# Attention rows of blocks 8 to 31 turned by DMA transposes of 16-bit halves

## The reference

```python
mod = (silu(c) @ wmod).reshape(2, 6, 1, 512)          # sa, ca, ga, sb, cb, gb
h = layernorm(x) * (1 + ca) + sa
q, k, v = silu(h @ wq), sigmoid(h @ wk), h @ wv         # 4 heads of 128
f = 1 - k;  g = log(f);  theta = cumsum(sign(f - 0.5)) * pi
S_t = S_(t-1) * exp(g_t) + k_t v_t;  o_t = (q_t * scale) S_t     # q and k times cos/sin(theta)
o = layernorm(o * sigmoid(h @ wg1 @ wg2)) * norm_w
x = x + ga * (o @ wo)
h = layernorm(x) * (1 + cb) + sb
xr, xk = mixes of h and of h one row earlier, by mu_r and mu_k
x = x + gb * sigmoid(xr @ W_r) * (square(relu(xk @ W_k)) @ W_v)
```

## Time and profile before

| | us |
|---|---|
| median of 3 runs | 1760.68 |
| lowest and highest | 1760.49, 1760.76 |
| profiled execution | 1760.39 |
| span of its instructions | 1758.6 |
| TensorE busy | 1736.2 |
| VectorE busy | 1544.2 |
| ScalarE busy | 905.6 |
| GpSimd busy | 409.2 |

### The profile page before, as it was taken

The page is one execution under the profiler, slowest core; times in us unless marked ns, Lnnn a source line. Parts: engine busy times, 40 slices in busy tenths (PEclk is TensorE's granted clock), DMA queues, the critical chain, the costliest instruction groups (busy, mean ns, idle before and its releaser), DMA issues.

```text
span 1758.6 us, 45285 instructions
## 1 busy us (share of the span) xinstructions
PE 1736.2 (99%) x18677; PEld 1559.8 (89%) x18677; DVE 1544.2 (88%) x3483; ACT 905.6 (51%) x1551; POOL 409.2 (23%) x361
## 2 busy tenths in 40 slices
PE   9999999999999999999999999998999999999999
PEld 7888989998999989999999989987788888888888
DVE  7898988998999989998989989898888888888885
ACT  4444444445444445444444444444566666666664
POOL 1000101101011011110111001101455555555552
PEclk9999999999999999999999999999999999999999
DMA  6122112211122111321112111121343332333331
GB/s 240 48 64 61 38 37 68 67 38 38 37 44 67 38 38 41 103 53 37 38 44 55 50 38 38 44 68 37 96 108 93 88 109 85 96 106 86 97 88 45
DMA packets 168949, 117.22 MB, mean 67 GB/s; under 512 B 126996, under 2 KB 128808, under 8 KB 168744
## 3 DMA queue, kind: packets, MB, share of 16 engines
q1 hardware_dynamic: 168728, 114.33, 24.6%
q10 hardware_dynamic: 16, 0.00, 0.0%
HBM read 48.77 MB, written 34.60 MB: 47 GB/s over the span
## 4 chain that ended last, share of the span: by engine, by line
PE 94%; DVE 5%; issue 1%; ACT 0%; DMA 0%; POOL 0%; SPq 0%; DVEq 0%; ACTq 0%
PE bank L1410 65%; PE lvl L1410 9%; PE bank L1517 3%; PE bank L1524 3%; PE bank L1516 3%; PE lvl L1485 3%; PE bank L1418 2%; PE bank L1508 1%; PE lvl L1468 1%; PE lvl L1503 1%; PE lvl L1497 1%; PE bank L1743 0%; DVE xn L139 0%; PE bank L1736 0%; DVE xk L1062 0%
## 5 line engine op out<-in xcount | busy, mean ns | idle before, releaser
L133 POOL TENSOR_TENSOR ln_rs<-ln_ve,mhalf 128x2 f32<-128x2 f32 x64 | 82.5, 1289 | 616.8 <-DVE ln_ve L128 616.6
L434 POOL COPY og_halves<-og 128x1024 uint16<-128x1024 uint16 x60 | 65.7, 1095 | 407.5 <-DVE og L1018 407.5
L1410 PE MATMUL bank<-xk_hi,fk_hi 128*128 128x256 f32 x512 | 145.8, 285 | 4.7 <-DVE xk_lo L1075 4.7
L1410 PE MATMUL bank<-hT_hi,wq_hi 128*128 128x256 f32 x512 | 148.2, 289 | 1.4 <-DVE hT_lo L821 1.2
L1410 PE MATMUL bank<-hT_hi,wk_hi 128*128 128x256 f32 x512 | 148.2, 289 | 0.0
L1410 PE MATMUL bank<-xk_lo,fk_hi 128*128 128x256 f32 x512 | 145.5, 284 | 0.0
L1410 PE MATMUL bank<-xk_hi,fk_lo 128*128 128x256 f32 x512 | 145.4, 284 | 0.0
L1410 PE MATMUL bank<-hT_hi,wq_lo 128*128 128x256 f32 x512 | 144.9, 283 | 0.0
L1410 PE MATMUL bank<-hT_lo,wk_hi 128*128 128x256 f32 x512 | 144.9, 283 | 0.0
L1410 PE MATMUL bank<-hT_lo,wq_hi 128*128 128x256 f32 x512 | 144.8, 283 | 0.0
L1410 PE MATMUL bank<-hT_hi,wk_lo 128*128 128x256 f32 x512 | 144.7, 283 | 0.0
(11 more groups left out here) (237 smaller groups left out, 5781.0 us busy)
## 6 DMA issues: line engine op xcount, KB each, us to landing
xs<-in_L_attn_x SPq DMA_DIRECT2D x32, 512.0 KB, 3.8
x_scratch<-xs SPq DMA_DIRECT2D x32, 512.0 KB, 3.4
xs<-x_scratch SPq DMA_DIRECT2D x32, 512.0 KB, 3.6
out<-xs SPq DMA_DIRECT2D x31, 512.0 KB, 2.8
mod_raw<-in_L_wmod SPq DMA_DIRECT2D x6, 1024.0 KB, 7.3
raw_q<-in_L_attn_wq SPq DMA_DIRECT2D x2, 512.0 KB, 4.7
raw_k<-in_L_attn_wk SPq DMA_DIRECT2D x1, 1024.0 KB, 5.7
raw_v<-in_L_attn_wv SPq DMA_DIRECT2D x1, 1024.0 KB, 6.7
```

Source lines behind the costliest of these rows:

```text
L133: pool.tensor_tensor(out=ln["rs"][:, :], in0=ln["ve"][:, :], in1=mhalf[:, :], op=ALU.pow).then_inc(ln["rstd"], 1)
L434: pool.tensor_copy(halves[:, ch, :].rearrange("p (two e) -> p two e", two=2), og[n % 2][:, ch, :].bitcast(U16).rearrange("p (e two) -> p t ...
L1410: last = pe.matmul(dst, lhs(a, s), rhs(b, s), start=(t == 0), stop=(t == len(terms) - 1))
```

## The change

The normalised rows of the blocks 8 to 31 (`FIRST_TURN <= n < NB`) are no longer turned by TensorE: body n leaves out `t1(n + 2)` for n = 6 to 29. ScalarE splits the two chunks of xn into 16-bit halves (`xn_split`), after the gate's first copy and before the keys' copies. SP issues two DMA transposes (`turn_rows`), ahead of `turn_og(n, 0)`. ScalarE joins the chunks into hF (`h_join`), behind the gate sigmoids, and scales hF in place (`h_scaled`). In these bodies VectorE makes the statistics before the level-32 update and no longer behind `q_odd`, and applies the normalisation behind the first totals and no longer behind `wo_scale`. In all bodies the scratch of `f_signed` is the first half of hF, and the wait on `mm["t1"]` before it is gone. The new tiles of halves lie where W_r's raw weights stood, so W_r is loaded in SP's iteration 30, after the last join. In the feed-forward part the turn by DMA begins one block later (n >= NB + 4): its block 3 is turned by TensorE in feed-forward body 2, behind the k rows, and scaled by `h2_affine`; GpSimd's split of it in body 1 is gone; and in body 2 VectorE's `apply_next` stands ahead of the low parts of ka.

```diff
@@ -145,9 +145,12 @@
     return n % BPB == 0
 
 
+FIRST_TURN = 8
+
+
 def by_dma(n):
 
-    return n >= NB + 3
+    return FIRST_TURN <= n < NB or n >= NB + 4
 
 
 def dma_before(n):
@@ -254,6 +257,8 @@
         halves = at("og_halves", [P, NC, 2 * E], 186, U16)
         halvesT = at("og_halves_turned", [P, NC, 2 * KT, P], 182, U16)
         raw_o2 = at("raw_o2", [P, KT, E], 190)
+        xn_halves = at("xn_halves", [P, NC, 2 * E], 198, U16)
+        xn_halvesT = at("xn_halves_turned", [P, NC, 2 * KT, P], 202, U16)
 
         raw = {name: at(f"raw_f{name}", [P, KT, E], kb) for name, kb in (("k", 190), ("r", 198), ("v", 190))}
         F = {name: [at(f"f{name}_{part}", [P, KT, E], kb + 8 * i, F32R) for i, part in enumerate(("hi", "lo"))]
@@ -354,6 +359,12 @@
                 mod_load(GA)
                 mod_load(GB)
 
+                def turn_rows(n, ch):
+
+                    sp.wait_ge(xn_halved, NC * dma_before(n) + ch + 1)
+                    wait(sp, xn_joined, NC * (dma_before(n) - 1) + ch + 1)
+                    sp.dma_start_transpose(xn_halvesT[:, ch, :, :], xn_halves[:, ch, :]).then_inc(xn_turned[ch], 16)
+
                 def turn_f(n, ch):
 
                     sp.wait_ge(xn_halved, NC * dma_before(n) + ch + 1)
@@ -375,7 +386,7 @@
                         wait(sp, x_out[n % 2], 16 * (n // 2))
                         sp.wait_ge(ln["stat"], n + 1)
                         ln_load(sp, ln, xf if n + 2 < NB else x2d, n + 2)
-                    if NB + 2 < n + 1 < 2 * NB:
+                    if NB + 3 < n + 1 < 2 * NB:
                         for ch in range(NC):
                             turn_f(n + 1, ch)
                     if n == 0:
@@ -393,11 +404,15 @@
                         rows_in(raw_o2, wod, wo2_in)
                     if n == BPB + 2:
                         sp.wait_ge(w_lo["o"], 2 * KT)
-                        for name in "kr":
-                            rows_in(raw[name], env["W_" + name], raw_in[name])
+                        rows_in(raw["k"], env["W_k"], raw_in["k"])
                     if n == LAST - 1:
+                        sp.wait_ge(xn_joined, NC * dma_before(NB))
+                        rows_in(raw["r"], env["W_r"], raw_in["r"])
                         sp.wait_ge(fw_lo["k"], KT)
                         sp.dma_start(raw["v"][:, :, :], env["W_v"].rearrange("(k p) n -> p k n", p=P)).then_inc(raw_in["v"], 16)
+                    if n + 2 < NB and by_dma(n + 2):
+                        for ch in range(NC):
+                            turn_rows(n + 2, ch)
                     if n < LAST - 1:
                         turn_og(n, 0)
                     if n > 0:
@@ -467,9 +482,6 @@
                             f_split(NB + m + 2, ch)
                     for ch in range(NC):
                         gate_b(m, ch)
-                    if m == 1:
-                        for ch in range(NC):
-                            f_split(NB + m + 2, ch)
                     for ch in range(NC):
                         add3(m, ch)
 
@@ -505,11 +517,33 @@
                 def h_affine(n):
 
                     act.wait_ge(h_lo, n) if n > 0 else None
+                    act.wait_ge(f_sb, 2 * n) if n > 1 else None
                     for k in range(KT):
                         if k % 2 == 0:
                             act.wait_ge(mm["t1"], 2 * pe_before(n) + k // 2 + 1)
                         src = bank[5 - 5 * (k // 2)][:, (k % 2) * TB:(k % 2 + 1) * TB]
                         act.activation(hF[:, k, :], src, ACT.Identity, scale=scl[0][:, n // BPB, k:k + 1],
+                                       bias=sft[0][:, n // BPB, k:k + 1]).then_inc(h_full, 1)
+
+                def xn_split(n, ch):
+
+                    act.wait_ge(ln["xn_ready"], n + 1)
+                    wait(act, xn_turned[ch], 16 * dma_before(n))
+                    act.copy(xn_halves[:, ch, :].rearrange("p (two e) -> p two e", two=2),
+                             xn[:, ch, :].bitcast(U16).rearrange("p (e two) -> p two e", two=2)).then_inc(xn_halved, 1)
+
+                def h_join(n, ch):
+
+                    act.wait_ge(xn_turned[ch], 16 * (dma_before(n) + 1))
+                    act.wait_ge(h_lo, n)
+                    act.wait_ge(f_sb, 2 * n)
+                    act.copy(hF[:, :, :].bitcast(U16).rearrange("p k (c t two) -> p c two k t", c=NC, two=2)[:, ch],
+                             xn_halvesT[:, ch, :, :].rearrange("p (two k) t -> p two k t", two=2)).then_inc(xn_joined, 1)
+
+                def h_scaled(n):
+                    act.wait_ge(xn_joined, NC * (dma_before(n) + 1))
+                    for k in range(KT):
+                        act.activation(hF[:, k, :], hF[:, k, :], ACT.Identity, scale=scl[0][:, n // BPB, k:k + 1],
                                        bias=sft[0][:, n // BPB, k:k + 1]).then_inc(h_full, 1)
 
                 def h2_affine(m, banks):
@@ -700,12 +734,20 @@
                     g1_high(n + 1)
                     if n == 0:
                         gate_copy(0, bank[3])
+                    if by_dma(n + 2) and n + 2 < NB:
+                        for ch in range(NC):
+                            xn_split(n + 2, ch)
                     for ch in range(chunks_kept(n)):
                         keys_turned(n, ch)
                     for ch in range(NC):
                         gate(n + 1, 1 - par, ch)
                     if n + 2 < NB:
-                        h_affine(n + 2)
+                        if by_dma(n + 2):
+                            for ch in range(NC):
+                                h_join(n + 2, ch)
+                            h_scaled(n + 2)
+                        else:
+                            h_affine(n + 2)
                     if n == 0:
                         gate_copy(1, bank[1])
 
@@ -750,10 +792,8 @@
                             square(m, pair)
                         for pair in range(2):
                             ka_high(m, pair)
-                    if m == 1:
+                    if m in (1, 2):
                         h2_affine(m + 1, TT)
-                    if m == 2:
-                        h2_scaled(m + 1)
                     for ch in range(NC):
                         r_sigmoid(m, ch)
                     if m + 1 < NB:
@@ -1188,22 +1228,28 @@
                         gate_wo2(n - BPB + KT)
                     if n == 5:
                         last_mods()
-                    dve.wait_ge(mm["t1"], 2 * (n + 2))
-                    f_signed(n + 1, 1 - par, 0, xn[:, 0, :])
+                    dma = by_dma(n + 2) and n + 2 < NB
+                    spare = hF[:, 0:2, :].rearrange("p k t -> p (k t)")
+                    f_signed(n + 1, 1 - par, 0, spare)
+                    if dma:
+                        ln_stats(dve, ln, n + 2)
                     if n == 1:
                         split_low_o(0, w_raw["o"], (0, 1))
                     if n == LAST - 1:
                         weight_low("k", [0])
                     level_update(n, par, 32, 4)
-                    f_signed(n + 1, 1 - par, 1, xn[:, 0, :])
+                    f_signed(n + 1, 1 - par, 1, spare)
                     if n == LAST - 1:
                         weight_low("k", [1])
                     q_odd(n + 1, 1 - par)
                     if n == 1:
                         split_low_o(0, w_raw["o"], (2, 3))
-                    ln_stats(dve, ln, n + 2)
+                    if not dma:
+                        ln_stats(dve, ln, n + 2)
                     ln_var(dve, ln, n + 2)
                     first_totals(n + 1)
+                    if dma:
+                        apply_next(n + 2)
                     level_update(n, par, 64, 5)
                     g1_low(n + 1)
                     first_update(n + 1, 1 - par)
@@ -1211,7 +1257,8 @@
                         weight_low("k", [2, 3])
                     if n > 0:
                         wo_scale(n - 1, 0, bank[3])
-                    apply_next(n + 2)
+                    if not dma:
+                        apply_next(n + 2)
                     variants(n + 1, 1 - par, 0)
                     if n == LAST - 1:
                         weight_low("r", [0])
@@ -1295,11 +1342,11 @@
                         shift(m + 1, "k")
                         if m + 2 < NB:
                             apply_next(n + 2)
+                    if m == 2:
+                        apply_next(n + 2)
                     if m > 1:
                         for pair in range(2):
                             ka_low(m, pair)
-                    if m == 2:
-                        apply_next(n + 2)
                     if m + 1 < NB:
                         if not early:
                             shift(m + 1, "k")
@@ -1626,7 +1673,8 @@
                         state_step(n, par, ch)
                     pe.wait_ge(kt_sb, kept(n, chunks_kept(n) - 1))
                     pe.wait_ge(gate_sb, 2 * (n + 1) + 1)
-                    t1(n + 2)
+                    if not by_dma(n + 2) or n + 2 >= NB:
```

(1 more changed line is left out.)

## The result

The changed kernel took 1739.74 us (median of 4 runs, 1739.65 to 1739.83), the kernel before 1760.59: a ratio of 0.9881, with a 95% interval from 0.9869 to 0.9893. The profiled execution took 1739.65 us, its span is 1737.9. The forecast was 1738.4 with a range from 1735 to 1746. So 20.85 us left the kernel where 22.3 were forecast. The terms were further off than the total: attention gave more, body 17 and the feed-forward part less.

The account below looks back on a forecast made before the run. The prediction took TensorE, busy 99% of the span, as the bound: 1760.4 - 19.0 (attention) + 0.6 (body 17) - 3.9 (feed-forward) = 1738.1; with the runs' median 0.3 higher, 1738.4 us, own range 1735.5 to 1741, wider range 1735 to 1746.

Parts of the forecast that it names:

- What bounds the kernel: Whole kernel: TensorE, busy 99% of the span and 94% of the chain; VectorE at 88% is the one to watch.
- TensorE in attention: Bodies turning blocks 8 to 31: eight transposes leave TensorE, 0.79 us each body, 24 x 0.79 = 19.0 us.
- VectorE, ScalarE and the queue: Turned attention bodies: earlier statistics and apply, splits and joins at 1.36 us, and landings of median 3.1 us all fit.
- The deadline: Turned attention bodies: hF's high and low parts end 1.3 us before TensorE reads them, 0.7 with a slow landing.
- Body 17: Attention body with 2.49 us more VectorE work: TensorE waits between 0 and 2.5 us, taken as 0.6.
- The ring: VectorE-ScalarE round into VectorE's next body: gaps about 1.0 us, slower from 1.8; rivals 1748 us (chance 0.07), 1775 (0.06).
- Feed-forward: Start of feed-forward body 3: wait 0.9 instead of 4.29 us, 3.9 us gained with the clock, bounds 0 and 4.8.
- upper bound of 3.62: Feed-forward body 2: VectorE's mix taken at 2.9 us, at most the 3.62 it took before beside GpSimd's multiplications.
- with so short a wait I expect the clock to stay up: Feed-forward body 3: after a wait of 0.9 us TensorE's clock stays up, 1.46 us more come back.
- The rule against the change: Turn by DMA: the skill gives 390 ns on TensorE, 1309 through the DMA crossbar, so the change would be a loss.

Follow-up runs that it names:

- The idle transposes: Changed kernel with eight transposes of the identity per body, read by nobody, put back on TensorE where the turn was: 1759.46 us.
- The runs with repeated splits: Changed kernel with each of ScalarE's splits made twice, the same values written again: 1744.88 us; made three times: 1797.71 us.
- the runs with the later multiplication: Changed kernel with GpSimd's gate multiplication in feed-forward body 2 held until the mixes are made: 1738.09 us; until the low part too: 1738.06 us.
- the run with the low parts apart: Changed kernel with half of body 17's low parts of the second output weights moved behind q_odd on VectorE: 1739.49 us.
- the late apply: Changed kernel with VectorE's statistics and normalisation back in their old places, the turn still by DMA: 1810.48 us.
- the apply behind ka: Changed kernel with VectorE's apply of feed-forward body 2 back behind the low parts of ka: 1739.69 us.

## Why the prediction was right, and where its terms were off

*What bounds the kernel* was right. The idle transposes show it: with 0.87 us per body of work given back to TensorE, the bodies return to 36.51 exactly.

*TensorE in attention* was mis-sized: 0.87 instead of 0.79. The eight starts and the start behind them were read (737.82 to 738.61), but the first transpose itself began later behind the state product than the output rows now do: 736.03 to 738.61 was 2.58 us, of which 1.71 remain. The right reading is from the start of the step ahead to the start of the step behind. 24 x 0.87 = 20.9 instead of 19.0.

*VectorE, ScalarE and the queue* held in kind. From the gap ahead of the level-32 update (723.61 - 1.96 = 721.65) to the apply's end the forecast has 729.3 - 721.65 = 7.65 us; from the statistics' start to the apply's end it took 720.35 - 712.87 = 7.48. A split was taken at 1.36 and is 1.05, a join took 1.34, as its row had said, and hF was whole 1.91 us after the start of the output rows (730.58 - 728.67), where the forecast has 739.9 - 737.82 = 2.08. The forecast of where the splits stand (between the first gate copy and the keys' copies) was right, with 1.05 us over instead of 0.2. The groups on ScalarE, for the earlier trace rows (count, busy us, mean ns, idle before):

```profile
L540 ACT COPY hF<-xn_halves_turned 128x1024 uint16<-128x1024 uint16 x48 | 61.2, 1341 | 1.7 <-DMA xn_halves_turned<-xn_halves 1.7
...
L532 ACT COPY xn_halves<-xn 128x1024 uint16<-128x1024 uint16 x48 | 47.9, 1048 | 2.6 <-DVE xn L139 2.5
```

The joins waited 1.7 us in all for the transfers, over 48 joins; their median landing is 3.2 us, against 3.1 for og.

*The deadline* was forecast with 1.3 us to spare, and 1.3 it is (732.87 to 734.18).

*Body 17* was forecast to lose 0.6 and lost 1.37 (37.01 - 35.64), inside its bounds of 0 and 2.5. The step that failed is the cover: the 1.3 us of slack at hT's deadline were counted for it, but TensorE waits for q_odd at the near scores, long before that deadline, where the cover was 1.17 us; and moving work past q_odd only moves the wait to the keys.

*The ring* was put at 1.0 us of gaps, and deciding from 1.8. The runs with repeated splits show 2.2, and so about 3.1. The gaps were added up one by one along the path with splits at 1.36; the shorter splits alone give back 0.6 of it. Whether the rest is VectorE's idle time before the last products (1.73 us at 727.16), which the sum left out, wasn't tried apart.

*Feed-forward* was the large error: 3.9 forecast, 1.2 measured. The turn on TensorE, the affine and the early dd came as described, and ka's low parts were in time (done at 1240.43, sooner than thought, since they ran in 1.29 us and not in 2.11). The failed step is the mix, taken at 2.9 us because GpSimd's multiplications would "overlap it less", where 5.18 was measured. With dd 2.9 us sooner (10.41 us after body 2's start instead of 13.27), the mix falls beside GpSimd's split of the next block, and then beside the multiplication as well. The four mixes end at 1242.74, 1243.91, 1245.34 and 1246.78; the four GpSimd instructions at 1242.46, 1243.64, 1245.06 and 1246.49. Each mix ends 0.28 us after one of GpSimd's: these four take turns with it, one for one. That isn't so throughout: GpSimd's first copy had stood since 1239.29 (3.17 us), while VectorE passed through the second ka low part and dd at 0.69 and 1.23 us. With the split alone beside them, in the runs with the later multiplication, the four mixes took 3.11 us. The forecast's upper bound of 3.62 came from a stretch where only two of GpSimd's instructions stood beside it, and was no bound.

The Trainium skill has this: "SBUF — State Buffer", section "Who interferes with whom", says that the ports which VectorE and GpSimd share are an exclusive lock, and that a VectorE instruction with two inputs in SBUF contends for them with a GpSimd instruction that reads SBUF. The trace agrees, with 1.14 to 1.51 us per mix against 0.47 alone. It had not been weighed in the forecast.

The second failed step of that part is "with so short a wait I expect the clock to stay up". With 2.13 us it fell. But the wait's length doesn't settle it: in the run with the low parts apart TensorE waited 2.12 us at the same place, and the clock stayed at 1.00:

```profile
1252.00:1253.00 1.00, 1.00 (x10) 1.00 (x9) 1.00 (x3) 1.00 (x2) 0.14 (x1) 1.00 0.00 0
```

Body 3 then took 16.77 us instead of 18.26, 1.49 less, near the 1.46 that the forecast had read from the two bodies. Seven traces have a wait of 2.10 to 2.13 us there: in five the clock fell and body 3 took 18.24 to 18.26, in two it stayed up (16.77, and 16.75 with the late apply). After 1.86 us (the apply behind ka) it fell, after 1.18 it didn't. So 1.5 of the forecast's 3.9 hung on something that the length of the wait doesn't decide; what does stays open.

*The rule against the change*, the Trainium skill's "VectorE: DVE Perf Modes", sections "Rules for kernel authors" and "The three transpose paths", ranks the DMA path as the slower one. The trace agrees on its length (3.2 us to land against 0.87 on TensorE) and disagrees on the outcome, a gain of 19.5 us in attention: the kernel pays for a path by what waits on it. The run with the late apply shows where the longer path is paid after all.

So the sum of 22.3 was 19.0 - 0.6 + 3.9; measured it is 20.9 - 1.4 + 1.2 = 20.7. That the total came out near owes something to errors of opposite sign.

## What to carry to other kernels

Where one engine is busy 99% of the time, a step that leaves it is worth its time from start of the step ahead to start of the step behind, as long as every engine of the longer path gets its input early enough; so move the producer forward first, and count the gaps of the ring. When an edit makes a VectorE step earlier, look at what GpSimd runs at the new time, not at the old one. A wait that is shortened may bring no more than its own microseconds: the stretch at the lower clock behind it goes only if the clock stays up. And the time of one execution says little about an edit worth 1 or 2 us: here the start and the clock differ by as much from trace to trace, so compare the stretch that the edit touches.

## What the runs showed of the hardware that was not expected

- ScalarE's copy of 1024 16-bit elements takes 1.05 us when it reads with a stride and writes densely, and 1.34 us when it joins halves with strided writes.
- VectorE and GpSimd held each other up instruction by instruction where the mixes stood beside GpSimd's copies and products: a mix of 256 columns takes 0.47 us alone and up to 1.51 beside GpSimd; GpSimd's split of two chunks took 4.35 us beside VectorE, where a like copy of one chunk takes 1.10.
- The granted clock fell to 1.2 GHz after an idle time of 1.86 us in one trace, and at the same place after 2.10 to 2.13 us in five traces of seven; in the other two it stayed up. After 3.47 or 3.48 us in the crossing it stayed down for nearly 6 us in one trace and was at 1.00 throughout in another.
